# A gated delta-rule layer on one core: norms kept as one number per token, Wo's product taken out of PSUM by VectorE, and a new order of the convolutions

## The reference, cut to what matters

```python
x = x + layernorm(attn(layernorm(x)))      # x: 8 x 1024 x 128
x = x + layernorm(ffn(layernorm(x)))

# attn: 16 heads, key size 64, value size 128, 4 taps
q = silu(conv4(x @ Wq.T)); k = silu(conv4(x @ Wk.T)); v = silu(conv4(x @ Wv.T))
q = q / max(|q|, 1e-6);    k = k / max(|k|, 1e-6)          # per token and head
alpha = exp(-exp(A_log) * softplus(x @ Wa.T + dt_bias)); beta = 2 * sigmoid(x @ Wb.T)
for t:  S = alpha_t * (S - beta_t * k_t (k_t S)) + k_t v_t;  o_t = S q_t
o = o * rsqrt(mean(o * o) + 1e-6)                           # per token and head
attn = concat_heads(o) @ Wo.T
```

## Time and profile before

| | |
|---|---|
| median of 3 runs | 4144.39 us (4143.23 to 4150.11) |
| the profiled execution | 4145.42 us, its span 4143.6 us |
| granted TensorE clock, mean | 0.972 |
| busy, share of the span | PE 77%, DVE 75%, ACT 75%, POOL 47% |

### The profile page before, as it was taken

One profiled execution on the slowest core, in us unless ns is written; L12 is line 12 of the kernel. 1 busy time (PEld: TensorE's weight loads), 2 busy tenths in 40 slices (PEclk: granted clock), 3 DMA queues, 4 the chain that ended last, 5 costly groups with the idle time before them and its releaser, 6 DMA issues. The chain is left out here.

```text
span 4143.6 us, 174764 instructions
## 1 busy us (share of the span) xinstructions
PE 3197.6 (77%) x69274; PEld 2242.2 (54%) x69274; DVE 3095.4 (75%) x5785; ACT 3095.9 (75%) x4524; POOL 1951.3 (47%) x3238
## 2 busy tenths in 40 slices
...
GB/s 61 55 51 59 52 58 53 58 53 58 53 58 53 57 54 56 55 57 55 55 56 52 60 52 60 51 61 50 61 50 62 49 62 49 60 51 60 41 38 46
DMA packets 911054, 226.07 MB, mean 55 GB/s; under 512 B 820128, under 2 KB 894112, under 8 KB 911008
## 3 DMA queue, kind: packets, MB, share of 16 engines
...
...
## 5 line engine op out<-in xcount | busy, mean ns | idle before, releaser
L826 DVE SCALAR_TENSOR_TENSOR cv<-ps,w_kq,cv 128x512 f32<-128x512 f32 x768 | 574.5, 748 | 523.7 <-ACT cv L712 505.5
L826 DVE SCALAR_TENSOR_TENSOR cv<-ps,w_v,cv 128x512 f32<-128x512 f32 x768 | 575.2, 749 | 247.0 <-ACT cv L712 233.4
L613 PE MATMUL ps<-Y,X 64*64 64x64 f32 x8192 | 179.4, 224 | 268.4 <-DMA X<-scrX 140.8
L786 ACT ACTIVATE Y<-ps 128x512 f32<-128x512 f32 x256 | 152.8, 597 | 275.6 <-PE ps L584 275.4
L642 PE MATMUL ps<-Rr,Z 64*64 64x128 f32 x4096 | 253.1, 272 | 126.0 <-ACT sq L758 125.1
L642 PEld LDWEIGHTS ps<-Rr,Z 64*64 64x64 f32 x4096 | 225.7, 133 | 228.4 <-issue 228.4
L955 POOL TENSOR_TENSOR ex<-ex,stP 128x512 f32<-128x512 f32 x128 | 133.9, 1046 | 437.0 <-ACT ex L719 437.0
L1003 POOL COPY XT<-NS 64x14 f32<-64x14 f32 x128 | 25.0, 195 | 628.2 <-DMA NS<-scrN 628.2
L627 PE MATMUL ps<-S,KB 64*64 64x128 f32 x4096 | 143.1, 277 | 220.9 <-DVE KT L855 220.9
L492 PE MATMUL ps<-xnT,w_kq 128*128 (+1 forms) x1024 | 305.3, 419 | 10.4 <-DVE cv L826 6.3
L613 PEld LDWEIGHTS ps<-Y,X 64*64 64x64 f32 x8192 | 151.4, 135 | 296.2 <-issue 296.1
...
## 6 DMA issues: line engine op xcount, KB each, us to landing
ex<-scrG SPq DMA_DIRECT2D x256, 128.0 KB, 2.8
scrN<-Nd SPq DMA_DIRECT2D x256, 128.0 KB, 2.4
Z<-scrZ SPq DMA_DIRECT2D x256, 128.0 KB, 2.9
X<-scrX SPq DMA_DIRECT2D x512, 64.0 KB, 2.4
w_kq<-wtab SPq DMA_DIRECT2D x128, 132.0 KB, 2.3
w_v<-wtab SPq DMA_DIRECT2D x128, 132.0 KB, 2.1
wo_s<-wo SPq DMA_DIRECT2D x128, 128.0 KB, 2.3
NS<-scrN SPq DMA_DIRECT2D x128, 64.0 KB, 2.5
```

The costliest lines, as they stand in the source:

```text
L613: last = nc.tensor.matmul(ps[a:z, col64((PAIR_B, PAIR_A)[l], cls, i)], BD["X" if l else "X0"][q, b * C:(b + 1) * C], BD["Y"][q, b * C:(b + ...
L786: nc.scalar.activation(two(half(BD["Y"], 0)), pair((PAIR_A, PAIR_B)[l]), ACT.Copy).then_inc(y_ok.sem, 1)
L826: nc.vector.scalar_tensor_tensor(cv4[:, j], pj[:, :, k:k + C], tap(j, k), cv4[:, j], ALU.mult, ALU.add).then_inc(conv.sem, 1)
```

## The change

**Norms as one number per token.** `pe_nk`, `pe_nq` and `pe_ms` use the squares as weights and one column of ones as the moving operand, so a norm is one number in a partition, in 8 columns for 8 batch elements. `gram_k`, `gram_p`, `ktr` and `ks` now read the keys and queries as they are after silu (`sl`). The key norm goes into the factors that were there already: `bn` (times beta, in `dmn`), `cr` (in `dve_r`), and `rv`, by which `act_v` scales V, in eight ACT instructions of 128x128. The query norm is folded into the output's own norm (`nqs`, `ro_in`). `dve_keys`, `dve_on`, `pool_qn`, two of the four table loads, and the 128x512 Relu, Ln and Exp instructions are gone.

**Wo.** `pe_wo` has the output as weights, so tokens are down the partitions. `dve_yr` takes the two banks out of PSUM times `ro`, and POOL adds them to the accumulator (`pool_acc`, two instructions). `act_osq` and `act_oc` read 1024 columns each. The feed-forward block reads the accumulator by four matmuls of 512 columns instead of eight of 128.

**Order.** Projections go keys, first V head, second V head, queries. `elim` and `sub` of step n are in the same pass as its `gram_k`. `XB` is written by ACT (`act_xb`). PE's queue has extra waits between its parts, since PSUM banks are laid out anew (`PB`). The tables are read in place, without the copies `stP` and `stR`.

The core of the diff (renamed semaphores, the removed functions and the bodies, whose order stands above, are left out):

```diff
--- before.py
+++ after.py
...
-ELIM = 14
-SUBS = 5
+ELIM = 13
+SUBS = 4
...
+        PB = {"dec": 4, "nk": 6, "gk": 2, "nq": 6, "gp": 6, "ktr": 2, "vtr": 4, "y0": 4, "z0": 2, "x": 4, "y1": 6, "z1": 4, "ks": 2, "u": 4, "o": 4, "ds": 6, "ms": 6, "wo": 2}
...
+                        last = nc.tensor.matmul(ps[place(cls, a), (PB["nk"] + cls) * 512 + i:(PB["nk"] + cls) * 512 + i + 1],
+                                                blk64(sq_kt, CLASSES[cls][i], a), k_all[a:z, K_BD + a:K_BD + a + 1],
+                                                start=True, stop=True)
...
+        def pe_nq(pe, n):
+            pe.wait_ge(sq_q.sem, sq_q.at(n))
+            pe.sem_inc(pe_go.sem, 1)
+            for i in range(4):
+                for h, (a, z) in enumerate(HALF):
+                    last = nc.tensor.matmul(ps[:, (PB["nq"] + h) * 512 + i:(PB["nq"] + h) * 512 + i + 1],
+                                            sq_qt[a:z, i * P:(i + 1) * P], k_all[a:z, K_BD + a:K_BD + a + 1], start=True, stop=True)
+            last.then_inc(nq_mm.sem, 1)
...
+            pe.wait_ge(osq_ok.sem, osq_ok.at(m))
+            pe.sem_inc(pe_go.sem, 1)
+                for i in range(4):
+                    last = nc.tensor.matmul(ps[:, (PB["ms"] + h) * 512 + i:(PB["ms"] + h) * 512 + i + 1],
+                                            osq[:, h * 512 + i * P:h * 512 + (i + 1) * P], kc(K_ONE, 1), start=True, stop=True)
+            last.then_inc(ms_mm.sem, 1)
+
...
+        def pe_wo(pe, m):
+            pe.wait_ge(oc_ok.sem, oc_ok.at(m))
+            pe.sem_inc(pe_go.sem, 1)
+                for i in range(4):
+                    last = nc.tensor.matmul(ps[:, col128(PB["wo"], h, i)], oo[:, h * 512 + i * P:h * 512 + (i + 1) * P],
+                                            wo_s[:, h * D:(h + 1) * D], start=True, stop=True)
+            act.wait_ge(proj[j].sem, proj[j].at(n))
+            nc.scalar.activation(cv4[:, j], pj[:, :, 0:C], ACT.Copy, scale=tap(j, 0)).then_inc(tap0[j].sem, 1)
+                                 bank(PB["dec"], 2).rearrange("p (g i n) -> p g i n", g=2, i=2), ACT.Exp).then_inc(dec_ex.sem, 1)
...
+            for b in range(NB):
+                last = nc.scalar.activation(unit(Vt, b), unit(ps, 4 * PB["vtr"] + b), ACT.Copy, scale=rv[:, b:b + 1])
+            last.then_inc(v_ok.sem, 1)
...
+        def act_osq(act, m):
+            act.wait_ge(o_mm.sem, o_mm.at(m))
+            if not first(m):
+                act.wait_ge(ms_mm.sem, ms_mm.at(m - 1))
+            nc.scalar.activation(osq[:], bank(PB["o"], 2), ACT.Square).then_inc(osq_ok.sem, 1)
...
+            nc.scalar.activation(oo[:], bank(PB["o"], 2), ACT.Copy).then_inc(oc_ok.sem, 1)
...
+        def act_rv_ln(act, n):
+            act.wait_ge(n2_ok.sem, n2_ok.at(n))
+            if not first(n):
+                act.wait_ge(v_ok.sem, v_ok.at(n - 1))
+            nc.scalar.activation(rv, n2, ACT.Ln).then_inc(rv_ln.sem, 1)
+
+        def act_rv_exp(act, n):
+            act.wait_ge(rv_ln.sem, rv_ln.at(n))
+            nc.scalar.activation(rv, rv, ACT.Exp, scale=-0.5).then_inc(rv_ok.sem, 1)
...
+        def act_xb(act, n):
+            act.wait_ge(sub.sem, sub.at(n))
+            if not first(n):
+                act.wait_ge(x_out.sem, x_out.at(n - 1))
+            nc.scalar.activation(XB[0:64, :].rearrange("g (j k) -> g j k", j=16), X16.rearrange("g k j -> g j k"),
+                                 ACT.Copy).then_inc(xb_ok.sem, 1)
...
+        def dve_yr(dve, m):
+            dve.wait_ge(wo_mm.sem, wo_mm.at(m))
+            dve.wait_ge(ro_ok.sem, ro_ok.at(m))
+            if not first(m):
+                dve.wait_ge(acc_ok.sem, acc_ok.at(m - 1))
+            for h in range(2):
+                last = nc.vector.tensor_tensor(yt[h].rearrange("p (i d) -> p i d", i=4),
+                                               bank(PB["wo"] + h).rearrange("p (i d) -> p i d", i=4),
+                                               ro[:, 4 * h:4 * h + 4].rearrange("p (i o) -> p i o", o=1).to_broadcast([P, 4, D]), ALU.mult)
...
+            nc.vector.tensor_scalar(n2.rearrange("p (g k) -> p g k", g=2), tiny(PB["nk"]), EPS_L2 * EPS_L2, None,
+                                    ALU.max).then_inc(n2_ok.sem, 1)
...
+            nc.vector.reciprocal(r2, n2).then_inc(r2_ok.sem, 1)
...
+            nc.vector.tensor_scalar(nqs.rearrange("p (g k) -> p g k", g=2), tiny(PB["nq"]), EPS_L2 * EPS_L2, EPS_RMS,
+                                    ALU.max, ALU.mult).then_inc(nqs_ok.sem, 1)
...
+            nc.vector.tensor_tensor(ro.rearrange("p (g k) -> p g k", g=2), tiny(PB["ms"]),
+                                    nqs.rearrange("p (g k) -> p g k", g=2), ALU.add).then_inc(ro_in.sem, 1)
...
+            nc.gpsimd.tensor_tensor(row(bn), tabP3[:, bass.ds(n, 1), 8:16], row(r2), ALU.mult).then_inc(bn_ok.sem, 1)
...
+            nc.gpsimd.tensor_tensor(row(cr), tabR3[:, bass.ds(n, 1), 0:8], row(r2), ALU.mult).then_inc(cr_ok.sem, 1)
...
+        def pool_acc(pool, m, h):
+            pool.wait_ge(yr_ok.sem, yr_ok.at(m))
+            if h or not first(m):
+                pool.wait_ge(acc_ok.sem, acc_ok.at(m, h))
+            pool.sem_inc(pool_go.sem, 1)
+            dst = acc3[:, bass.ds(m % NC, 1), :]
+            nc.gpsimd.tensor_tensor(dst, dst, row(yt[h]), ALU.add).then_inc(acc_ok.sem, 1)
```

More of the change, by code:

```diff
@@ L99, in build @@
         wo_s = sb("wo_s", 2 * D)
-        stP = sb("stP", 24)
-        stR = sb("stR", 16)
+        sc = sb("sc", 64)
         Lm = sb("Lm", 2 * 512)
@@ L364, in build @@
         dmp_ok = sig("dmp_ok")
-        proj = sig("proj", 4)
-        tap0 = sig("tap0", 4)
-        conv = sig("conv", 12)
+        proj = [sig("proj_" + k) for k in ("k", "q", "v0", "v1")]
+        tap0 = [sig("tap0_" + k) for k in ("k", "q", "v0", "v1")]
+        conv = [sig("conv_" + k, 3) for k in ("k", "q", "v0", "v1")]
         silu_k = sig("silu_k")
@@ L435, in build @@
         CLASSES = (range(0, 4), range(4, 8))
-        PAIR_A, PAIR_B, PAIR_C = 2, 4, 6
+        r0r1, u_mms, u_oks, s_oks = (r0_ok, r1_ok), (u0_mm, u1_mm), (u0_ok, u1_ok), (s0_ok, s1_ok)
+        osq = BD["KB"]
+        yt = (half(BD["X"], 1), half(BD["Y"], 1))
+        n2, r2, rv, bn, cr, nqs, ro = (sc[:, 8 * k:8 * k + 8] for k in range(7))
+        row = lambda t: t.rearrange("p (o k) -> p o k", o=1)
+        acc3 = accT[:].rearrange("p (c k) -> p c k", k=512)
+        PB = {"dec": 4, "nk": 6, "gk": 2, "nq": 6, "gp": 6, "ktr": 2, "vtr": 4, "y0": 4, "z0": 2, "x": 4, "y1": 6, "z1": 4, "ks": 2, "u": 4, "o": 4, "ds": 6, "ms": 6, "wo": 2}
         def tap(j, k):
@@ L539, in pe_gram_p @@
                     for a, z in HALF:
[L540 to L550 removed]
+                        kb = blk64(sl, CLASSES[cls][i], a)
+                        last = nc.tensor.matmul(ps[place(cls, a), col64(PB["gk"], cls, i)], kb, kb, start=True, stop=True)
+            last.then_inc(gram_k.sem, 1)
+        def pe_gram_p(pe, n):
+            pe.wait_ge(silu_k.sem, silu_k.at(n))
+            pe.wait_ge(silu_q.sem, silu_q.at(n))
             pe.sem_inc(pe_go.sem, 1)
```

691 lines of the change are left out of this document (364 added, 327 removed).

## The result

The changed kernel takes 3859.01 us, the median of four runs (3857.67 to 3863.06), against 4143.85 us for the kernel before on the same chip: a ratio of 0.9311, 95% interval 0.9295 to 0.9327. That is 118 us above the 3741 us of the forecast and inside its range. The span went from 4143.6 to 3855.9 us. 127 periods, from the first to the last `XB` copy, take 27.31 us each. The same periods of the kernel before take 29.72 (the 62 passes of the earlier trace rows had 29.68): 306 us saved. Outside the loop 3855.9 - 127 x 27.31 = 388 us are left against 4143.6 - 127 x 29.72 = 369, so 19 us were lost there.

What follows compares the result with a forecast made beforehand. No engine is full; waits between engines, so their order, bound the 29.68 us pass. DVE's queue closes at 26.3, plus 0.2 makes 26.5: 4145 - 127 x (29.68 - 26.5) = 3741 us, range 3620 to 3930.

Steps and rivals of the forecast that it cites:

- DVE passed over twice: At L871 and L878 DVE waits through two POOL instructions; 1.2 us more, 27.3 to 28.5 a pass; rival, chance 0.17.
- The clock was taken as 2.4 GHz throughout: PE's clock in the loop: read as 0.99, the 2.4 GHz level, before; no term for a change of it.
- The pass of 26.5 at full clock: DVE's queue from `conv0` through `r`, `n`, `conv3`, `conv1`, `sub`, `s0` closes at 26.3 us; 0.2 added for the layout's shortfall.
- the way through DRAM: `Nd` through DRAM to POOL and `elim`: 10.3 us, hidden by 0.2 before; after the change it has most of a pass.
- the sign that I named for the DRAM way: POOL's `XT` copy released by `NS` later than DVE's `nqs` would show that the DRAM ring decides.
- Contention: DVE's `sub` running under POOL work throughout: 1.1 us charged for L871 and 0.35 for L878 a pass.
- L871 at 1.5 to 2.0: Sign of being right: this DVE instruction in `sub` takes 1.5 to 2.0 us under POOL work, 0.68 when POOL is idle.
- starved: DVE's L871 waits until POOL is idle; 31.8 us a pass, 4412 us in all; slower rival, chance 0.04.
- contention stays small: POOL lets DVE in at once, `ms` costs 1.0; ACT's ring decides, 25.3 to 25.9 us, 3590 to 3665; rival, chance 0.13.
- The rival that charged 0.1 for each of some twenty: PE's waits each drain its queue, 0.1 us exposed each; 28.5 to 29.4 a pass, 3995 to 4110; chance 0.06.
- The ACT ring: From the end of `o` to the next, through V's pieces, taps, convolutions, `u`: 25.5 us, within 1 us of DVE's.
- The small products on PE: `nk`, `nq`, `ms` as one-column products, mostly weight loads: `ms` 1.4 us, between 1.06 and 2.05; `nk` and `nq` 0.6 each.
- Outside the loop: The accumulator's read in the feed-forward block, hidden but once: taken as 0, within 10 us both ways, of 374 us.

Runs made afterwards that it cites:

- e2_all64: The changed kernel with the one-column products `nk`, `nq` and `ms` streaming 64 columns each; 3749.1 us, ratio 0.8995 to the kernel before.
- e7_all64_late_sg: The changed kernel with 64 columns in `nk`, `nq`, `ms`, `ms` moved between `y0` and `z0`, POOL's `Sg` products ahead of `elim`; 3590.2 us, ratio 0.8607.
- e8_late_sg_vone: e7_all64_late_sg with V copied by one ACT instruction instead of eight, leaving out V's division by the key norm; 3581.9 us, ratio 0.8595.

## Why the prediction was right in its direction and 118 us off

The gap is 127 x (27.31 - 26.5) = 103 us in the loop and 14 outside it (388 where the forecast had 374).

The measured time lies outside the band of the forecast proper (26.0 to 27.2 a pass, 3678 to 3830), to which the prediction gave 0.60. It lies in the band of a rival, DVE passed over twice (3845 to 3995), and that rival did not come (below). So it was partly luck that the stated range took the time in: its upper end was held open for another reason, and neither the sum nor any rival had a change of the clock.

**The clock was taken as 2.4 GHz throughout**, as the earlier trace rows had it for the kernel before. This is the step that failed. The change makes `ms` a row of weight loads with one column each, and the granted clock of the loop fell from 0.99 to 0.90. With nothing but the columns of `ms` widened to 64, the mean pass is 26.52, the forecast's 26.5. By the spans (3855.9 and 3755.6) it is 100 us of the 118; by the ratios, which take the chip out, 3.1% of 4144, 130 us, more than the whole gap. The prediction named PE busy above 24 as a sign of being wrong, and the sign came: 896.64 of 1000 us are 24.5 a pass, where the undisturbed pass has 22.67.

**The pass of 26.5 at full clock was right in part by luck.** I closed it through DVE's queue: contention of 1.1 on L871 (now L921) and 0.35 on L878 (now L928), and 0.4 of wait for `sg`. At full clock L921 is undisturbed (0.68), and DVE idles 1.55 us ahead of `s1`, for `ds`, so DVE's queue didn't bind. (L928 takes 1.22 there, so 0.2 of the 0.35 charged to it were paid.) The ring that did is POOL's with the DRAM way, and one that is near to mine lies 0.44 below it. I had its pieces: `r` waiting for `cr`, `Nd` behind `ms`, and the way through DRAM covered by only 0.2. I took them one at a time and never added them up to a ring: 26.34. Nor could the sign that I named for the DRAM way show it: POOL's `XT` copy comes 3.9 us ahead of `nqs` (2048.62 and 2052.52 in e2_all64), but `elim` behind it ends together with `nqs`. Two readings of the earlier trace rows were also small: `r` is 2.15 in its row, not 2.06, and the Z copy 1.19, not 1.1.

**Contention** was charged to DVE, 1.1 and 0.35 us. In the changed kernel L921 takes 1.08 on the mean (0.67 to 1.57) where it was 0.68 alone, so 0.40, and L928 1.09 against 1.0. The sign "L871 at 1.5 to 2.0" didn't come. Who pays depends on who starts first: in the rows above POOL had begun 0.06 us ahead of L921 (2004.73), which took 1.52; in e2_all64 L921 begins 0.03 ahead of POOL and takes 0.68, and POOL's instruction 1.80. In the changed kernel DVE began first in 30 of the 128 steps, and L921 took 0.67 to 0.68 in each of them. POOL pays more: the mean of one in the changed kernel is 1.38 for `Sg` (1.03 in e7_all64_late_sg, where it stands ahead of `elim`), and 1.40 and 1.65 for the two of `acc` (1.27 alone), in all 2 x 0.35 + 0.13 + 0.38 = 1.2 us a pass. As POOL was in the binding ring, that share counted. The Trainium skill, "GPSIMD Engine Reference", section "Specifications", says that the two share their SBUF interfaces, with contention where a DVE instruction has two SBUF inputs; the rows agree, and show either engine waiting. The rivals in which DVE is passed over twice, or starved, did not come: L921 never took more than 1.57, where being passed over twice took 2.89. That in which contention stays small has its 25.3 to 25.9 a pass only in the experiments, with the columns widened and pieces taken out of POOL's ring (25.14 to 25.95). Of PE's gates two stand out in the steady pass of e2_all64: 0.20 ahead of `ms`, which is in the ring, and 0.99 ahead of `dec`, for V's copy on ACT. The rival that charged 0.1 for each of some twenty, 28.5 and more a pass, did not come.

**The ACT ring** was worked out as 25.5, with V's pieces at 2.90. They take 2.13 for eight (one takes 363 ns, and they overlap), so that sign didn't come either; why the same form took 2.90 in the feed-forward block was not looked into. `XB` took 0.63 (0.5 taken), the 8-column instructions 0.21 (0.30). With 2.13 the sum of 25.5 would be 24.7, and the steady pass with POOL's ring cut is 25.14, so either is within 0.45 of it; but that ACT's ring sets it isn't shown (e8_late_sg_vone).

**The small products on PE.** `ms` took 1.84 to 1.92, not 1.4, and `nk` and `nq` 0.64 and 1.06, not 0.6 each. For `ms` the step chose the middle of 1.06 and 2.05 where it belonged near the upper end. The Trainium skill, "TensorE: Matmul & The Clock Gate", section "LDWEIGHTS (loading the stationary operand)", by its P / 1.2 ns gives an estimate of 1.7 for 16 loads, nearer than mine. `ms` was in the ring, so what it took beyond 1.4 counted; the 0.3 us by which I said the pass would then be longer can't be told from the terms that came out lower.

**DVE's tiny instructions** took 0.16 to 0.20, as charged; the two holes ahead of `conv3` and `conv1` 0.84 and 0.86, as forecast (0.8). ACT's busy time is 17.6 a pass (18.5), DVE's 20.1 (20.6 and contention). PE's is 22.67 in the undisturbed pass (22).

**Outside the loop** I took 0, within 10. It was 14 against my 374, and 19 by like periods. The accumulator's read (L1568) takes 29.4 us, and the wait for it, in the changed kernel and then in the kernel before:

```profile
DVE small L1469 <- PE ps L1568: 43.5, 8, 5.7
```
```profile
DVE small L1346 <- PE ps L1443: 27.9, 8, 3.8
```

The 15.6 us more are near the size of the loss. From the first read to the end of the kernel it is 202.0 us before and 221.5 after, so the whole loss lies there. The clock has a share in it: over that stretch it was 0.75 before and 0.68 after, and PE is busy 106.9 and 132.9 us, 26 more, of which the read itself makes only 29.4 - 14.9 = 14.5. How the loss divides between the two wasn't tried. With the columns of `ms` widened it stays: from the last `XB` copy to the end it is 258 to 262 us in every kernel with the new read, and 239 to 241 in those with the old. I had counted columns of the moving side and called all but one of eight reads hidden; the wait shows that each of the eight was on the path.
